# Two graph layers: four count buffers, the further-edges check moved behind the dense products, the degrees on POOL's queue, and the self loops' diagonal added by VectorE

## The reference, cut to what matters

```python
# x [2500, 1024], src and dst [80000] sorted by dst, edge_weight [80000]
h = relu(layernorm(x))
x = x + segment_sum((h @ W0)[src] * edge_weight[:, None], dst)      # first layer
h = relu(layernorm(x))
row, col = concat(src, arange(2500)), concat(dst, arange(2500))     # self loops appended
deg = zeros(2500).at[row].add(1.0)
norm = deg[row] ** -0.5 * deg[col] ** -0.5
x = x + segment_sum(norm[:, None] * (h @ W1.T + b)[col], row)       # second layer
```

## Time and profile before

| what | value |
|---|---|
| median of 3 runs | 1526.2 us (1524.74 to 1527.38) |
| profiled execution | 1524.97 us |
| its span, first to last instruction | 1523.2 us |
| granted TensorE clock, mean | 0.991 |
| PE busy | 1436.6 us, 94% |
| DVE busy | 912.0 us, 60% |
| ACT busy | 522.7 us, 34% |
| POOL busy | 522.6 us, 34% |

### The profile page before, as it was taken

How to read it: one execution, slowest core, us unless ns; L and a number is a source line. 1 busy time by engine, 2 the same in 40 slices (tenths; PEclk the granted TensorE clock), 3 DMA queues, 4 the chain that set the end, 5 groups by cost and what they waited for, 6 DMA issues and landing times.

```text
span 1523.2 us, 24189 instructions
## 1 busy us (share of the span) xinstructions
PE 1436.6 (94%) x7586; PEld 845.3 (55%) x7587; DVE 912.0 (60%) x1644; ACT 522.7 (34%) x922; POOL 522.6 (34%) x1025
## 2 busy tenths in 40 slices
PE   3989999999889899999999999899999999999999
PEld 2445555456555566666666666345546546446455
DVE  7788885635666676666666673586452452452442
ACT  7545655423444445555555551430000000000000
POOL 2246664625556666666666661000000000000000
PEclk9989999999999999999999999999999999999999
DMA  8302542252333443545354548654507208108002
GB/s 301 111 20 46 119 97 30 26 120 46 63 63 70 85 78 71 103 82 94 70 102 83 93 80 181 206 137 94 153 1 179 68 2 204 43 12 208 29 1 81
DMA packets 427813, 139.10 MB, mean 91 GB/s; under 512 B 397705, under 2 KB 409993, under 8 KB 427669
## 3 DMA queue, kind: packets, MB, share of 16 engines
q1 hardware_dynamic: 427669, 137.43, 40.3%
HBM read 53.46 MB, written 53.52 MB: 70 GB/s over the span
## 4 chain that ended last, share of the span: by engine, by line
PE 41%; issue 20%; POOL 16%; DVE 8%; ACT 4%; DMA 4%; POOLq 3%; SPq 2%; ACTq 2%; DVEq 0%
PE pair L1870 18%; PE pair L1930 13%; POOL deg_acc L778 7%; PE pair L1783 5%; PE pair L1670 4%; POOL area L785 3%; DVE own_w L1350 2%; ACTq L1397 2%; DMA deg_scratch<-deg 2%; POOLq L757 1%; ACT area L1404 1%; DMA x_scratch<-xt 1%; ACT area L1405 1%; POOL fbuf L760 1%; PE pair L1682 1%
## 5 line engine op out<-in xcount | busy, mean ns | idle before, releaser
L1783 PE MATMUL pair<-h,area 128*128 128x512 f16 x2400 | 547.6, 382 | 21.6 <-issue 20.8
L1783 PEld LDWEIGHTS pair<-h,area 128*128 128x128 f16 x2400 | 342.0, 147 | 183.1 <-issue 36.0
L1870 PE MATMUL pair<-area,h 128*128 128x500 f16 x1600 | 341.6, 377 | 11.0 <-DVE h L1287 8.0
L1870 PEld LDWEIGHTS pair<-area,h 128*128 128x128 f16 x1600 | 157.1, 98 | 194.7 <-issue 16.6
L1410 ACT ACTIVATE aux<-area 128x320 f16<-128x320 f32 x144 | 125.0, 868 | 268.1 <-POOL area L785 207.9
L1930 PE MATMUL pair<-wmat,area 128*125 128x512 f16 x960 | 210.7, 382 | 2.4 <-DVE area L1330 2.4
L1042 DVE TENSOR_TENSOR slots<-iota_r,fbuf 128x320 f16<-128x320 f16 (+1 forms) x145 | 101.3, 699 | 175.3 <-POOL fbuf L772 128.5
L790 POOL TENSOR_TENSOR aux<-area,aux 128x320 f16<-128x320 f32 x144 | 144.7, 1005 | 173.4 <-ACT aux L1410 173.4
L1604 ACT ACTIVATE area<-pair,sc 128x500 f16<-128x500 f32 x40 | 27.1, 677 | 448.6 <-PE pair L1870 448.6
L1930 PEld LDWEIGHTS pair<-wmat,area 128*125 128x125 f16 x960 | 131.8, 138 | 78.7 <-issue 4.5
L778 POOL TENSOR_TENSOR deg_acc<-deg_acc,area 128x320 f32<-128x320 f32 x160 | 144.1, 901 | 46.2 <-ACT area L1405 43.6
(11 more groups left out here) (208 smaller groups left out, 1296.8 us busy)
## 6 DMA issues: line engine op xcount, KB each, us to landing
c_scratch<-aux SPq DMA_DIRECT2D x72, 320.0 KB, 4.4
xt<-in_x SPq DMA_DIRECT2D x19, 512.0 KB, 3.5
x_scratch<-xt SPq DMA_DIRECT2D x19, 512.0 KB, 4.7
xt<-x_scratch SPq DMA_DIRECT2D x20, 448.0 KB
out_x<-xt SPq DMA_DIRECT2D x19, 448.0 KB
h<-x_scratch SPq DMA_DIRECT2D x4, 2048.0 KB, 13.3
h<-in_x SPq DMA_DIRECT2D x5, 1024.0 KB, 7.3
h<-in_L_gnn_W SPq DMA_DIRECT2D x4, 1024.0 KB, 11.1
```

The costliest lines, as they stand in the source:

```text
L1783: last = pe.matmul(sum_pair(e)[:, half * H:(half + 1) * H], wts(e)[:, q, :, k], hpart(k, r)[:, half * H:(half + 1) * H], start=k == q == r ...
L1870: ins = pe.matmul(sums_of(c, f), hpart(k, q)[:, f * P:(f + 1) * P], counts, start=first and q == 0, stop=last and q == 1, skip_group_check ...
```

## The change

It has five parts.

1. `c_stage` gets four buffers instead of two (CST = 4). ACT's `window_out` now waits for `c_lo` of the quad four back instead of two back. The two buffers more lie where the early stage had its parked parts, so ACT waits once, before the main loop, until those are stored.
2. With them the orders change: ACT does `window_out` of quad n first and `counts_first` of quad n - 1 after it. POOL does the degree sum of quad n and then `counts_left` of quad n - 1. In the early stage POOL makes the next fields before `counts_left`.
3. DVE adds the diagonal (in `second_part`, ahead of L1110) instead of POOL. POOL's degree sum waits for it (`c_self`) and so includes the self loop; the `+ 1.0` of the degree goes.
4. PE's check for further edges stands behind the dense products instead of ahead of them.
5. The degrees' store and load are issued by POOL at its program's end instead of by SP between the loads of x1.

```diff
+        early_second = area[:, PARK + SW:PARK + 3 * SW // 2].bitcast(f16)
         def second_of(s):
-            a = PARK + SW if s == 0 else PARK
+            a = STG + 4 * SW + s * SW // 2
...
+        CST = 4
...
             for k in range(4):
                 sp.wait_ge(sup_free, k + 1)
                 load_x1(k)
-                if k == 1:
-                    sp.wait_ge(deg_ready, 1)
-                    sp.dma_start(deg_dram.rearrange("t p -> p t"), deg[:, 0:T], ...).then_inc(deg_out, 16)
-                    sp.wait_ge(deg_out, 16)
-                    sp.dma_start(deg[0:RW, T:2 * T], flat[0:N].rearrange("(t p) -> p t", p=RW), ...)
...
             def sum_counts(n, s):
-                pool.wait_ge(win_act, n + 1)
+                pool.wait_ge(c_self, n + 1)
                 need(pool, win_sum, n)
                 pool.tensor_tensor(deg_acc[:], deg_acc[:], c_stage(s), ALU.add).then_inc(win_sum, 1)
-            def add_self(n, s, td, q):
-                pool.wait_ge(more_consts, 3)
-                pool.wait_ge(win_sum, n + 1)
-                own = by_source(c_stage(s))[:, bass.ds(td, 1), :]
-                pool.tensor_tensor(own, own, half_ident[...].unsqueeze(1), ALU.add).then_inc(c_self, 1)
...
-            def counts_of(n, s, td, q):
-                sum_counts(n, s)
-                add_self(n, s, td, q)
+            def counts_of(n, td, q, first=False):
+                sum_counts(n, q % CST)
+                if not first:
+                    last_left(n - 1, (q - 1) % QPT)
+            def last_left(n, q):
                 at = slice(q % QH * RQ, (q % QH + 1) * RQ)
                 half = c_half(q // QH)
-                counts_left(n, s, half[:, 0, :, at], half[:, 1, :, at])
+                counts_left(n, q % CST, half[:, 0, :, at], half[:, 1, :, at])
...
                     if w > 0:
-                        early_counts_of(w - 1)
+                        early_sum(w - 1)
                     if w + 1 < PQ:
                         fields_of(w + 1)
...
+                    if w > 0:
+                        early_left(w - 1)
...
+            last_left(NQ - 1, QPT - 1)
+            pool.wait_ge(deg_ready, 1)
+            pool.dma_start(deg_dram.rearrange("t p -> p t"), deg[:, 0:T], ...).then_inc(deg_out, 16)
+            pool.wait_ge(deg_out, 16)
+            pool.dma_start(deg[0:RW, T:2 * T], flat[0:N].rearrange("(t p) -> p t", p=RW), ...).then_inc(degu_in, 16)
...
-            def second_part(n, s, r, parts, seconds, pair):
+            def second_part(n, r, parts, seconds, pair, counts, td, q):
                 dve.wait_ge(win_act, n + 1)
+                own = by_source(counts)[:, bass.ds(td, 1), :]
+                nc.vector.tensor_tensor(own, own, half_ident[:, q * RQ:(q + 1) * RQ].unsqueeze(1), ALU.add).then_inc(c_self, 1)
                 nc.vector.scalar_tensor_tensor(by_window(parts[:, 1], r), sums_in(pair, r, 1), A_DOWN,
                                                by_window(parts[:, 0], r), ALU.mult, ALU.subtract).then_inc(win_evac, 1)
...
-                chain(nc.vector.tensor_scalar(deg[:, 0:T], deg[:, 0:T], 1.0 / C_DOWN, 1.0, ALU.mult, ALU.add))
+                chain(nc.vector.tensor_scalar(deg[:, 0:T], deg[:, 0:T], 1.0 / C_DOWN, None, ALU.mult))
...
-                need(act, c_lo, n - 1)
+                need(act, c_lo, n + 1 - freed)
...
                     if q == 0:
                         act.wait_ge(agg_ready, td)
+                    window_out(n, q % CST, r, CST, quad_of(1 - e, q)[:, 0], second_of(q % 2), win_pair(q % 2))
                     if q > 0 or before:
                         p = (q - 1) % QPT
-                        counts_first(n - 1, (q - 1) % 2, c_half(p // QH)[:, 0, :, p % QH * RQ:(p % QH + 1) * RQ])
-                    if q % QH == 0:
-                        b = q // QH
-                        act.wait_ge(c_out[b], (32 * PQ if b == 0 else 0) + 32 * (td + 1 - PRE))
-                    window_out(n, q % 2, r, td, quad_of(1 - e, q)[:, 0], second_of(q % 2), win_pair(q % 2))
+                        b = p // QH
+                        if p % QH == 0:
+                            act.wait_ge(c_out[b], (32 * PQ if b == 0 else 0) + 32 * (td + 1 - PRE))
+                        counts_first(n - 1, p % CST, c_half(b)[:, 0, :, p % QH * RQ:(p % QH + 1) * RQ])
...
             act.wait_ge(table_ready, 2)
+            act.wait_ge(c_lo, PQ)
+            act.wait_ge(a_out, 32 * PQ)
+            act.wait_ge(c_out[0], 32 * PQ)
...
                         own_step((2 * i + e + 1) * 4 + g // 2 + QB // 2 + PRE_STEPS - PQ, g // 2 % 2, 4, pair, g % 2)
+                    dense(i, e, g, SUMS_EARLY)
                     further(n, row_n, pair)
-                    dense(i, e, g, SUMS_EARLY)
```

39 lines of the change are left out of this document (21 added, 18 removed).

## The result

The changed kernel takes **1507.6 us** (median of 4 runs, 1501.9 to 1511.1), the kernel before 1525.5 in the same session: ratio 0.9883, 95% interval 0.9863 to 0.9904, so 18 us faster. The forecast was 1485 us, 41 less than before. The time lies just inside the range (1469 to 1508); more than half of the forecast gain is missing.

The account below looks back on a forecast made before the run. It took a POOL and ACT ring to bound narrow tiles, and PE plus its check for further edges the wide ones. Terms -22 - 12 - 4 - 3 = -41 took 1526.2 to 1485 us, range 1469 to 1508.

Parts of the forecast that it names:

- Degrees on POOL's queue: Behind the main loop: SP's 23.6 us wait between x1 loads goes, later loads come earlier; -4 us, ends -13.8 and +15.
- Early stage: Before the main loop: POOL's fields no longer stand behind ACT's part of the quad before; -3 us, ends 0 and -8.
- Narrow tiles, -22: Main loop's six narrow tiles: each falls from 35.0 to 31.3 us; -22 us, ends -35 and no gain.
- The round of 3.81: Narrow tiles: new ring of fields, one-hots, diagonal, sum and remainder takes 3.81 us a quad, against 4.00 before.
- the old ring through ACT: Narrow tiles before: POOL and ACT wait in turn, 4.00 us a quad; the eighth round takes 7.0 at a tile's border.
- The check behind the dense products: Twelve wide tiles: the check's 0.46 us, open after steps PE waited for, gets hidden; -12 us, ends 0 and -14.6.
- stores of single elements run beside SP's transposing loads and hold them up: Rival behind the loop: POOL's degree stores delay SP's loads or come too late for DVE; +15, so 1500 us; 4%.
- ACT's three new waits: Before the main loop: they cost nothing, standing in the 26 us in which PE does a tile's products alone.
- Diagonal costs DVE nothing in wide tiles: Wide tiles: DVE's 0.1 to 0.2 us a quad is covered by its idle time; without that cover 14 us.
- The rival by the SBUF lock: Narrow tiles: L1113 goes between POOL's sum and remainder, 0.25 a round, making 4.06; some 1500 us; 20%.
- PE is the bound: Rival for the whole main loop: rounds overlap more than seen, so PE bounds it everywhere; 1470 us; 9%.
- the check behind the products is covered: Against it, a rival: 0.46 us stands open in all 144 quads, wide tiles 32.9 us; 1536 us; 7%.

## Why the prediction was wrong, point by point

Two steps failed: "Degrees on POOL's queue", -4, measured +14.1, and "Early stage", -3, measured +7.8. In both the forecast's sum left out what the edit does to SP's queue. The two terms of the main loop had the right size, one of them for half the right reason.

- **Narrow tiles, -22.** Right: -24.9. The round of 3.81 measured 3.76, diagonal, sum and hop as priced. It was right also that the old ring through ACT stops at the border and the new one hardly does; but the round falls by the diagonal alone, and the border by buffers and orders.
- **"The check behind the dense products", -12 in the wide tiles.** The sum was right (-12.3), the reason only half, and so the size was in part luck: in the finished kernel the late check brings nothing in the wide tiles (29.2 us with it and without) and 3 us in the narrow ones. The late check alone brings the wide tiles to 29.5 to 30.8; the diagonal on DVE alone brings all of them to 29.2; with the diagonal on POOL, buffers, orders and late check together take all as well. Several edits remove the same stall, and the last one in finds nothing left. The forecast said itself that the 0.46 stands open only behind a step that PE had to wait for the earlier trace rows, and then removed the 0.46 and not the wait. A shorter ring takes the wait away, and the check is covered again.
- **"Early stage", -3.** Failed. It was priced from PE's waits alone. Fields ahead of the remainder were counted as a gain; that the remainder is therefore late, and that SP's queue stands at its head for it with W1's stores and x's loads behind, was not looked at, though SP's waits of before show it, 123.0 us in 15, in a stretch of which the forecast read PE's waits only. Measured +7.8 in the profiled spans: +5.0 of PE's idle time, of which 3.9 go when the order is undone (4 us by ratios), and +2.8 of busy time at a lower granted clock. The mechanism of the gain was right and larger than thought: 17 us with the queue free.
- **"Degrees on POOL's queue", -4.** Failed, and with it the largest part of the error. What was forecast to come back did, and more of it (9.6 us behind the first count product, 6.8 of them idle time of PE), but the stretch up to the first count product grew by 23.7, all of it PE's first wait (7.1 to 30.7). The rival named it, "stores of single elements run beside SP's transposing loads and hold them up", with +15 and 4%; the stage came out at +14.1. That the numbers meet is luck: the rival worked its +15 out from degrees that come too late for DVE at t == 8, and DVE has no such wait in the changed kernel; it is PE's first wait that pays. The mistake is the chance, and that the hold-up had no price of its own: SP's queue had kept those transfers apart by its order: before, the element store is issued at 946.42, behind the transposing loads (930.99 to 944.13) and the first two loads of x1, and after it starts at 897.79, 8.8 us behind the last own step and just ahead of them (900.51). I asked what the removed wait frees and not what the moved transfer would meet.
- **At nothing: ACT's three new waits.** Right; PE has no gap where the main loop starts.
- **Diagonal costs DVE nothing in wide tiles.** Right, 29.18 a tile.
- **The rival by the SBUF lock.** It fell. L1122 did grow to 0.71. The Trainium skill (SBUF — State Buffer, "Who interferes with whom") says that a DVE instruction with two SBUF inputs contends with a GpSimd one that reads SBUF. L1122 took 0.70 at the median of the narrow tiles, where L1113 had taken 0.32, so this trace agrees that the two meet. But the round paid some 0.05, not 0.25: it was DVE that stood, and DVE had 1.14 of idle time behind it in the rounds of this timeline.
- **The others.** PE is the bound in the wide tiles and not in the narrow ones; the check behind the products is covered in all 144 quads.

With the two failed terms at what they measured, the forecast's sum would have been -22 - 12 + 14 + 8 = -12, against -15.3 in the spans and -17.8 in the medians.

**What stays open.** With the diagonal on DVE and the old order the main loop starts at 350.1, 354.9, 355.2 and 355.4 in four kernels, and at 347.2 to 352.6 without it. PE's idle time up to there is 40.4 to 41.9 us in the four and 39.3 before, so the diagonal's share of the idle time is 1 to 3 us at most. The rest is PE's busy time, 309.6 us where the start is 350.1 and 313.4 to 314.5 in the other three; why the granted clock differs between them (0.99 against 0.97 to 0.98) is not known. Why the degrees on POOL cost the kernel before 7 us and the changed one 13 wasn't tried; the traces show only that the element store took 17.9 us to landing there and 24.4 here, and the five transposing loads 28.77 us and 36.41. Whether elements on a second queue hurt because they are elements wasn't tried either.

## What to carry to other kernels

A transfer that moves to another queue must be costed by what will be in flight beside it at its new time, not only by what stood behind it in its old queue; the transfer of single 4-byte elements was a bad neighbour here on POOL's queue and on ACT's, and hardly one behind the loads on their own queue. When an engine's order is turned so that something comes later, read the in-order queue whose head waits for it, the one that issues the stores above all, and move what stands behind it ahead: the same reordering was worth -17 us with that and some +4 without. And when several edits take away the same stall, run each alone before naming the one that pays: here one small move gave 28 of the 37 us, and the edit that the profile's idle row pointed at gave 3 in the finished kernel.

## What the runs showed of the hardware

- Two transfers of 2,560 and 2,500 elements of 4 bytes (10.0 and 9.8 KB; 24.4 and 15.5 us to landing) stretch five transposing loads that run beside them from 13.1 to 36.4 us when POOL issues them, to 28.2 when ACT's hardware queue does. With POOL issuing the store 3.4 us behind the first load of x1 instead, those loads took 32.4 us to landing (17.2 in the changed kernel). Issued by SP behind the first two loads of x1, the same store left these at 13.8 and 14.1 us (13.0 without it in flight, 25.4 with it on POOL's queue).
- A DVE add (L1122) that started while POOL's sum ran took 0.70 at the median of the narrow tiles instead of 0.32; POOL's next instruction began before it ended and took 1.03 instead of 0.98. The price of the overlap fell on DVE.
- The check's place costs nothing where no step is waited for: wide tiles have the same 29.18 us with it ahead of the dense products and behind them.
- TensorE, idle from 921.4 to 952.2, had a granted clock of 0.50 (the 1.2 GHz level) from 926.7 to 957.3 and 1.00 after that; its count products started 0.42 us apart at the one and 0.21 at the other.
